# Retention layer: its first projections in float32 and rotated from PSUM, fillers moved, q's high half one step later, the last batch's two outputs two steps apart

## The reference

```
# B=8 batches, L=32*32 tokens, E=256, 8 heads of 32; x normalised by groups
q = xf @ Wq.T;  k = (xf @ Wk.T) * 32**-0.5;  v = xf @ Wv.T
qr = q * cos + rotate_every_two(q) * sin      # kr the same from k
qk = einsum('bhqd,bhkd->bhqk', qr, kr) * mask
den = clip(abs(qk).sum(-1), 1, 50000)
out = layernorm_per_head(einsum('bhqk,bhkd->bhqd', qk / den, v))
x = x + gelu(out) @ Wo.T
```

## Time and profile before

| | us |
|---|---|
| median of 3 runs | 2418.2 |
| lowest and highest | 2412.84, 2422.38 |
| the profiled execution | 2417.03 |
| its span, first to last instruction | 2415.2 |
| PE busy in it | 2365.0 (98%) |
| DVE, ACT, POOL busy | 1783.8, 1466.0, 1011.7 |

### The profile page before, as it was taken

The page is one execution under the profiler, slowest core; times in us unless marked ns, Lnnn a source line. Parts: engine busy times, 40 slices in busy tenths (PEclk is TensorE's granted clock), DMA queues, the critical chain, the costliest instruction groups (busy, mean ns, idle before and its releaser), DMA issues.

```text
span 2415.2 us, 38886 instructions
## 1 busy us (share of the span) xinstructions
PE 2365.0 (98%) x14998; PEld 1662.0 (69%) x14998; DVE 1783.8 (74%) x2769; ACT 1466.0 (61%) x2097; POOL 1011.7 (42%) x735
## 2 busy tenths in 40 slices
PE   8999999999999999999999999999999999999999
PEld 4444444444444444999899778888888888888887
DVE  6788878788878777677766667767777766677775
ACT  3777777777777777566565455555555554555554
POOL 3788988888888885134232101111111111001110
PEclk8999999999999999999999999999999999999999
DMA  6344444444444443255455310000000000000000
GB/s 222 76 100 105 88 106 88 107 104 106 103 107 97 95 113 91 73 75 94 78 92 85 84 51 21 27 27 27 27 27 27 27 27 27 27 27 9 18 27 18
DMA packets 89272, 164.78 MB, mean 68 GB/s; under 512 B 21744, under 2 KB 63096, under 8 KB 80768
## 3 DMA queue, kind: packets, MB, share of 16 engines
q1 hardware_dynamic: 80016, 96.23, 15.1%
q0 software_dynamic: 9072, 66.06, 13.6%
HBM read 70.95 MB, written 25.26 MB: 40 GB/s over the span
## 4 chain that ended last, share of the span: by engine, by line
PE 86%; DVE 4%; POOL 3%; issue 3%; ACT 2%; DMA 1%; another core or an unknown queue 0%; SPq 0%; DVEq 0%; ACTq 0%; POOLq 0%
PE scores L1838 10%; PE scores L1840 10%; PE scores L1839 10%; PE scores L445 8%; PE pairC L473 8%; PE pairC L492 4%; PE pairD L374 4%; PE pairC L1838 2%; PE pairC L1839 2%; PE pairC L1840 2%; PE pairD L1838 2%; PE pairD L1840 2%; PE pairD L1839 2%; PE pairD L383 2%; PE pairD L423 2%
## 5 line engine op out<-in xcount | busy, mean ns | idle before, releaser
L610 DVE TENSOR_TENSOR l_prod<-scores,l_window 128x1024 f32<-128x1024 f32 x512 | 603.1, 1220 | 177.3 <-PE scores L445 172.1
L810 ACT ACTIVATE l_absp<-l_prod 128x1024 f32<-128x1024 f32 x512 | 523.1, 1052 | 173.7 <-PE pairC L492 86.4
L1997 ACT ACTIVATE e_r<-scores,e_bn,e_rs 128x512 f32<-128x512 f32 x256 | 197.9, 779 | 276.4 <-PE scores L1840 276.3
L2228 POOL TENSOR_TENSOR e_xnorm<-e_res,e_scale 128x1024 f32<-128x1024 f32 x16 | 38.6, 2415 | 775.5 <-DMA e_res<-t2T_scratch 775.5
L967 POOL TENSOR_TENSOR l_absp<-l_absp,l_absp 128x1024 f32<-128x1024 f32 x126 | 298.8, 2394 | 12.1 <-ACT l_absp L810 12.1
L2104 DVE CAST e_h1hi<-e_r 128x512 fp32r<-128x512 f32 x256 | 144.9, 566 | 208.6 <-ACT e_r L1997 208.3
L2007 ACT ACTIVATE e_r<-scores,e_bn,e_rs 128x512 f32<-128x512 f32 x250 | 195.0, 781 | 137.8 <-PE scores L1840 136.4
L473 PE MATMUL pairC<-l_prod,l_v 128*32 128x512 f32 x2048 | 274.5, 608 | 0.0
L2131 DVE TENSOR_TENSOR e_r<-e_r,e_wbc 128x512 f32<-128x512 f32 x250 | 170.8, 691 | 86.0 <-ACT e_r L2007 85.8
L2106 DVE TENSOR_TENSOR e_h1lo<-e_r,e_h1hi 128x512 fp32r<-128x512 f32 x256 | 208.4, 814 | 8.8
L445 PEld LDWEIGHTS scores<-l_qhi,l_khi 32*128 32x128 f32 x1024 | 61.7, 182 | 221.0 <-DVE l_prod L610 132.1
(11 more groups left out here) (284 smaller groups left out, 5299.4 us busy)
## 6 DMA issues: line engine op xcount, KB each, us to landing
l_absp<-l_absp POOLq DMA_DIRECT2D x63, 1024.0 KB, 7.3
l_xo<-in_x SPq DMA_DIRECT2D x32, 256.0 KB, 2.7
x_scratch<-l_xo SPq DMA_DIRECT2D x32, 256.0 KB, 4.9
l_xa<-x_scratch SPq DMA_DIRECT2D x8, 1024.0 KB, 8.4
l_xr<-x_scratch SPq DMA_DIRECT2D x8, 1024.0 KB, 5.5
t2T_scratch<-l_xt SPq DMA_DIRECT2D x8, 1024.0 KB, 14.6
e_scale<-rows_scratch SPq DMA_DIRECT2D x16, 512.0 KB, 4.1
e_res<-t2T_scratch SPq DMA_DIRECT2D x16, 512.0 KB, 5.0
```

Of the source, the lines that this page charges most:

```text
L610: nc.vector.tensor_tensor(prod[2 * (S % 2) + j][:], sc[j][:], win[:, 4 * g + 2 * j:4 * g + 2 * j + 2, w0:w0 + QC], ALU.mult).then_inc(prod ...
L810: nc.scalar.activation(absp[S % ABS][j][:], prod[2 * (S % 2) + j][:], ACT.Abs).then_inc(abs_ready, 1)
L1997: nc.scalar.activation(r1[:, m, :], p1[m], ACT.Relu, bias=bn_[0][1][:, m, n:n + 1], scale=rs[0][:, m, n:n + 1]).then_inc(r1_ready, 1)
```

## The change

The opening's three projections and the q and k projections of phase 0 become `project_whole`: one float32 matmul for each half of the 256 inputs, straight on `xn`, `wk_in` and `wq_in`. So they need no halves of x and of the weights. The low parts of x are made later by POOL (`x_low`, four instructions), after K1's low half and ahead of the first pair; the low parts of the weights (`weights_low`) by POOL at the start of phase 1, and PE waits for both ahead of the q projection of phase 1. DVE shuffles K0 and Q0 straight from their banks and reads the bank for the cosine product too; ACT copies only K1. The six fillers ahead of the first scores are gone, and one filler, written to the bank den, stands behind them, with a wait for K1's copy.

In every phase ACT makes q's high half at the end of step 3 instead of step 2, and POOL issues the pair of step 2 ahead of q's low half instead of behind it. In phase 30 the first output stands whole in the first part of step 4, the second at step 6 instead of 5, and its residual (`add_residual`) at step 7 instead of 6.

```diff
             if before == "k":
-                pe.wait_ge(first_taken, K0 + 1)
+                pe.wait_ge(first_cos, K0 + 1)
...
+        def project_whole(w, g, c, parts, to=pA, done=a_ready):
+
+            for k in parts:
+                mm = nc.tensor.matmul(to[:], w[:, k, 128 * g:128 * g + 128], xn[:, k, QC * c:QC * c + QC],
+                                      start=(k == 0), stop=(k == 1))
             if 1 in parts:
                 mm.then_inc(done, 1)
...
             if n == 0:
-                pe.wait_ge(first_taken, K1 + 1)
+                pe.wait_ge(first_taken, 1)
...
-        def busy(count):
+        def busy(count, to=sc[1][:, 0, :]):
...
             for n in range(count):
-                nc.tensor.matmul(sc[1][:, 0, :], prod[3][:, 1, 0:128], prod[3][:, 1, :], start=True, stop=True)
+                nc.tensor.matmul(to, prod[3][:, 1, 0:128], prod[3][:, 1, :], start=True, stop=True)
 
         busy(7)
         pe.wait_ge(weights_in, 16 * NWEIGHTS)
@@ -504,18 +512,19 @@
         busy(1)
         group_sums(gvar[:], gvar_ready, 1)
         busy(1)
-        pe.wait_ge(w_lo, 2)
-        pe.wait_ge(xlo_ready, 2)
-        project(wkhi, wklo, 0, 0, (0, 1))
-        project(wqhi, wqlo, 0, 0, (0, 1), pB, first_made)
-        pe.wait_ge(xlo_ready, 4)
-        project(wkhi, wklo, 0, 1, (0, 1), den, first_made)
+        pe.wait_ge(high_made, 1)
+        pe.wait_ge(first_xn, 2)
+        project_whole(wk_in, 0, 0, (0, 1))
+        project_whole(wq_in, 0, 0, (0, 1), pB, first_made)
+        pe.wait_ge(first_xn, 4)
+        project_whole(wk_in, 0, 1, (0, 1), den, first_made)
         pe.wait_ge(wv_centred, 2)
         project_v(0, 0, (0, 1), num, first_made)
-        pe.wait_ge(first_taken, Q0 + 1)
+        pe.wait_ge(first_cos, Q0 + 1)
         project_v(0, 1, (0, 1), pB, first_made)
-        busy(6)
         scores(0)
+        pe.wait_ge(first_taken, 1)
+        busy(1, den)
         pe.wait_ge(consts, 16 * NCONST)
...
             if kt == 0 and has_q(P):
                 if part == 0:
                     a_free(("q", P))
-                project(wqhi, wqlo, (P + 1) // 2 % 2, (P + 1) % 2, (part,))
+                if P == 0:
+                    project_whole(wq_in, 0, 1, (part,))
+                else:
+                    if P == 1 and part == 0:
+                        pe.wait_ge(w_lo, 2)
+                        pe.wait_ge(xlo_ready, 4)
+                    project(wqhi, wqlo, (P + 1) // 2 % 2, (P + 1) % 2, (part,))
...
-                project(wkhi, wklo, G % 2, half, (part,))
+                if P == 0:
+                    project_whole(wk_in, 1, 0, (part,))
+                else:
+                    project(wkhi, wklo, G % 2, half, (part,))
...
             if kt == 4 and outs(P):
-                out_proj(*outs(P)[0], (part,))
+                if len(outs(P)) == 1:
+                    out_proj(*outs(P)[0], (part,))
+                elif part == 0:
+                    out_proj(*outs(P)[0], (0, 1))
...
-            if kt == 5 and len(outs(P)) == 2:
+            if kt == 6 and len(outs(P)) == 2:
                 out_proj(*outs(P)[1], (part,))
...
-        def first_x_low():
-
-            for n in range(4):
...
         def first_shuffle(n):
 
-            dve.wait_ge(first_taken, n + 1)
+            source, ready, count = ((pA, a_ready, 3), (pB, first_made, 1), (first_t1[K1], first_taken, 1))[n]
+            dve.wait_ge(ready, count)
             dve.sem_inc(waited, 1)
-            nc.vector.stream_shuffle(first_t2[n], first_t1[n], [i ^ 1 for i in range(32)]).then_inc(first_shuffled, 1)
+            nc.vector.stream_shuffle(first_t2[n], source[:], [i ^ 1 for i in range(32)]).then_inc(first_shuffled, 1)
 
         def first_rotate(n):
 
+            nc.vector.tensor_tensor(rows(first_t1[n]), rows((pA, pB)[n][:]), turn(cos_sb, 0), ALU.mult).then_inc(first_cos, 1)
             dve.wait_ge(first_shuffled, n + 1)
             nc.vector.tensor_tensor(rows(first_t2[n]), rows(first_t2[n]), turn(sin_sb, 0), ALU.mult).then_inc(first_sine, 1)
-            nc.vector.tensor_tensor(rows(first_t1[n]), rows(first_t1[n]), turn(cos_sb, 0), ALU.mult).then_inc(first_cos, 1)
             dve.wait_ge(first_sine, n + 1)
             dve.wait_ge(first_cos, n + 1)
             nc.vector.tensor_tensor(first_t1[n], first_t1[n], first_t2[n], ALU.add).then_inc(first_sum, 1)
...
         first_normalise()
-        first_x_low()
         centre_values()
...
-            if kt == 6 and len(outs(P)) == 2:
+            if kt == 7 and len(outs(P)) == 2:
                 add_residual(*outs(P)[1])
...
-        def first_take(n):
-
-            bank, ready, count = ((pA, a_ready, 3), (pB, first_made, 1), (den, first_made, 2))[n]
-            act.wait_ge(ready, count)
-            nc.scalar.activation(first_t1[n], bank[:], ACT.Copy).then_inc(first_taken, 1)
+        def first_take():
+
+            act.wait_ge(first_made, 2)
+            nc.scalar.activation(first_t1[K1], den[:], ACT.Copy).then_inc(first_taken, 1)
...
-        first_take(K0)
-        first_take(Q0)
-        first_take(K1)
+        first_take()
         first_v(0)
         act.wait_ge(first_sum, K1 + 1)
         nc.scalar.activation(first_high[K1], first_t1[K1], ACT.Copy).then_inc(first_hi, 1)
...
             if kt == 2 and P > 0:
                 squares(P - 1)
-            if kt == 2 and has_q(P):
+            if kt == 3 and has_q(P):
                 high(prep_q(P))
...
-        pool.wait_ge(high_made, 2)
-        nc.gpsimd.tensor_tensor(wqlo[:], wq_in[:], wqhi[:].bitcast(F32), ALU.subtract).then_inc(w_lo, 1)
         group_rstd(0)
-        pool.wait_ge(high_made, 3)
-        nc.gpsimd.tensor_tensor(wklo[:], wk_in[:], wkhi[:].bitcast(F32), ALU.subtract).then_inc(w_lo, 1)
         pool.wait_ge(tables_in, 16 * NTABLES)
         pool.wait_ge(first_shuffled, K1 + 1)
...
+        x_low(0, 0)
+        x_low(0, 1)
+
+        def weights_low():
+
+            pool.wait_ge(high_made, NHIGH)
+            pool.wait_ge(a_ready, a_order["k", 0] + 1)
+            nc.gpsimd.tensor_tensor(wqlo[:], wq_in[:], wqhi[:].bitcast(F32), ALU.subtract).then_inc(w_lo, 1)
+            nc.gpsimd.tensor_tensor(wklo[:], wk_in[:], wkhi[:].bitcast(F32), ALU.subtract).then_inc(w_lo, 1)
+
         for P in range(PHASES):
+            if P == 1:
+                weights_low()
             if P > 0:
                 pair(P - 1, 6)
...
             if has_q(P):
                 rotate(prep_q(P), (P + 1) % 2)
                 rotated(prep_q(P))
+            pair(P, 2)
+            if has_q(P):
                 low(prep_q(P))
-            pair(P, 2)
             if P > 0:
                 scale_heads(P - 1)
             pair(P, 4)
```

7 lines of the change are left out of this document (2 added, 5 removed).

## The result

| us | before | after |
|---|---|---|
| median, 6 runs each | 2416.9 | 2403.4 |
| lowest and highest | 2412.84, 2422.38 | 2399.88, 2405.52 |
| profiled execution | 2417.03 | 2403.11 |

The ratio is 0.9942 with an interval of 0.9926 to 0.9959: the changed kernel is 0.6% faster. The forecast was 2403 us, with a sum of 2403.1 for the profiled execution. So the total fits to a tenth of a microsecond. The steps don't all fit as well, and two of them need experiments.

The account below looks back on a forecast made before the run. It took the opening's single chain with fillers before the scores, half-clock stretches and phase 2's ACT wait for POOL as bounds; -7.7 - 2.6 + 0.3 + 0 - 3.9 + 0 = -13.9 from 2417.0 gave 2403 us, range 2398 to 2411.

Parts of the forecast that it names:

- Part 1: Opening up to the first scores: earlier projections and no six fillers, scores at 24.2 instead of 31.92, -7.7 us.
- the half-clock end: Opening's first projection with PE at half clock: it lasts 3.5 us and the shuffle comes at 16.8, against 15.2 at full.
- Parts 2 and 3: First two steps at full clock with one filler between their scores, -2.6 us; phase 0's k projection in float32, +0.3 us.
- Part 4: POOL's new splits of x and weight differences before phase 1's q projection fit its free time: 0, ends 0 and +2.4.
- Part 5: Phase 2: q's high half a step later, its low half behind the pair, -3.9 us; other phases 0.
- Part 6: Phase 30: second output and its residual one step later, 0, ends -0.5 and +0.5 us.
- (a): Rival: the clock falls again in the first steps, +3.4 us on the sum, 2406.5; chance 0.18.
- (b): Rival: phase 2 stays slow, from POOL's late sum or other waits lowering the clock, 2407; chance 0.14.
- (d): Rival: POOL, 1.0 us later, becomes the bound; some 30 phases each grow by 0.6 us, +18, 2421; chance 0.05.

Follow-up runs that it names:

- The filler experiment: Changed kernel with the six old fillers back ahead of the first scores in place of the new one behind them: 2407.7 us, ratio 0.9973.

## Why the prediction was right, step by step

**Part 1, the opening, was undersized:** -9.3 us by the profiles, against -7.7 and an end of -8.7. POOL's power (forecast 10.9, measured 10.97) and PE's first projection (13.1 and 12.87) were right. The shuffle was put at 16.2 and came at 15.00. I chose nearer to the half-clock end, by the row at half clock in the earlier trace rows; the clock was full throughout, and that end gives 15.2. The rest of those 1.2 us, 0.2, is DVE: the sum took the 2.87 us of the four pieces over unchanged, while the same part of the change removed POOL's instruction that had made them 0.95 us longer. The chain from the shuffle to q's low half took 22.55 - 15.00 = 7.55 us, not 8.0: the cosine reads the bank and starts at 15.62, ahead of the shuffle's end at 15.73, where it had stood behind the sine. Part of the 9.3 us isn't the change's: the opening of the kernel before took 21.39 us in the one profile and 20.62 in the other, by where its clock was halved, so with the second one the gain is 8.5. PE was not what held the scores: V's last matmul ends at 22.14, forecast 21.9 at full clock. The filler experiment shows 4.6 us of the part as a cause; the rest is read from rows.

**Parts 2 and 3** were right: steps 0 and 1 took 30.91 - 23.68 = 7.23 us for a forecast of 7.3, phase 0 is 2.28 us shorter for 2.3, the step with k's projection went from 3.71 to 4.04 us (+0.33 for +0.3). That the filler is what holds the clock was an argument; the kernel without it bears it out, in one profile.

**Part 4** was right with 0. POOL is busy for 18.5 us of the 22 from 42 to 64, and its last weight difference ends at 53.5, 2.2 us ahead of PE's q projection at 55.77. Phase 1 has the same 28.47 us.

**Part 5** had the right size in phase 2 by the wrong step, which is luck. The forecast took away a wait and with it the clock's fall as its consequence. The runs show 0.8 to 1.1 us for the wait and 3.0 for the fall, and the fall hangs on more than the wait: with the part undone behind the new opening it didn't come, and in the kernel before with one filler it didn't either. So in the changed kernel as it stands the part is worth 0.8 us in the trace, and the two medians with and without it (2402.4 and 2402.2) show nothing; alone in the kernel before it gives 3.0 us of median, 2410.8 for 2413.8. What decides whether the fall comes behind a given starved stretch stays open: PE had been busy for 5.27 and 5.47 us of 7 ahead of the two falls, and for 5.25 and 5.32 of 7 where the clock held. The forecast also named the earlier issue of the pair and gave it 0 in the other phases, since nothing waits for ACT there; but PE waited for that DMA in a few of them, and this is worth 0.5 to 1.3 us. The forecast added part 1 and part 5 as if each brought its own gain, and they share the 3 us.

**Part 6** was right with 0, and so, within what the profiles show, was the judgment that ACT's 50.2 us of waits cost nothing outside phase 2.

**The rivals.** (a) and (b) didn't come; the runs without the filler and with phase 2 as it was put them at +1.6 and +0.8 us in this kernel, and the forecast had +3.4 and +3.9, since it took the price of a fall from the longest one seen. (d) didn't come either, and the delay that was forced on POOL, three times (d)'s, worked mainly by another chain.

The whole was right to 0.4 us of the median, with errors of both signs in it: 1.6 us too little for the opening, 0.9 for the phases from 3 on, and 2.8 us behind the layer, mostly chance, that took back what the layer had gained beyond the sum. So the fit to the last tenths was luck.
